# Attention values for two heads at a time, on 64 columns each, with the softmax sums added up on GpSimd

## What is computed

```python
scores = jnp.einsum('bqhd,bkhd->bhqk', q, k) * scale
attn = jax.nn.softmax(scores, axis=-1)
out = jnp.einsum('bhqk,bkhd->bqhd', attn, v)
out = out.reshape(b, t, N_HEADS * HEAD_DIM)
return out @ Wo.T
```

## Time and profile before

| | |
|---|---|
| median of three runs | 1585.21 us (1584.91 to 1586.8) |
| the profiled execution | 1585.56 us, of which the span is 1583.7 us |
| TensorE products busy | 1303.0 us, 82% of the span |
| VectorE busy | 1131.1 us, 71% |
| ScalarE busy | 755.4 us, 48% |
| GpSimd busy | 551.9 us, 35% |

### The profile page before, as it was taken

One profiled execution on the slowest core, in us unless ns is written; L12 is line 12 of the kernel. 1 busy time (PEld: TensorE's weight loads), 2 busy tenths in 40 slices (PEclk: granted clock), 3 DMA queues, 4 the chain that ended last, 5 costly groups with the idle time before them and its releaser, 6 DMA issues. The chain is left out here.

```text
span 1583.7 us, 23730 instructions
## 1 busy us (share of the span) xinstructions
PE 1303.0 (82%) x5791; PEld 914.4 (58%) x5792; DVE 1131.1 (71%) x2460; ACT 755.4 (48%) x1490; POOL 551.9 (35%) x952
## 2 busy tenths in 40 slices
PE   6499999999999999999999999999941254969600
PEld 3266666666666666666666666666631154869500
DVE  2368777788787777877788787777627784556487
ACT  1366556565565655656565565654410023333135
POOL 1101314133242323414233241322340055766548
PEclk8699999999999999999999999999955555989855
DMA  4000010110101101010110101101012012223275
GB/s 111 14 14 28 2 54 11 43 53 0 54 0 53 54 0 53 0 54 25 29 54 0 53 0 41 42 2 41 33 61 60 1 53 70 38 50 71 27 251 173
DMA packets 68357, 70.26 MB, mean 44 GB/s; under 512 B 13568, under 2 KB 64176, under 8 KB 68160
## 3 DMA queue, kind: packets, MB, share of 16 engines
q1 hardware_dynamic: 46336, 46.92, 9.9%
q10 hardware_dynamic: 16896, 16.78, 3.2%
q0 software_dynamic: 5056, 5.85, 2.4%
HBM read 40.35 MB, written 28.92 MB: 44 GB/s over the span
## 5 line engine op out<-in xcount | busy, mean ns | idle before, releaser
L824 PE MATMUL PS<-PF,V 128*128 128x512 f32 x1024 | 523.9, 593 | 0.0
L555 ACT ACTIVATE PF<-PS 128x512 f32<-128x512 f32 x512 | 303.3, 596 | 344.5 <-PE PS L750 342.9
L727 DVE TENSOR_REDUCE NMAX<-PS 128x1 f32<-128x512 f32 x512 | 346.6, 687 | 161.9 <-PE PS L759 151.8
L749 PE MATMUL PS<-Q,K 128*128 128x512 f32 x512 | 405.7, 792 | 0.9 <-ACT PF L555 0.9
L525 POOL TENSOR_TENSOR XL<-XF,XH 128x512 fp32r<-128x512 f32 x64 | 84.4, 1318 | 446.7 <-ACT XH L630 446.7
L759 PE MATMUL PS<-K,Q 128*128 128x512 f32 x512 | 203.3, 398 | 6.5 <-DVE NMAX L727 6.0
L750 PE MATMUL PS<-Q,K 128*128 128x512 f32 x512 | 202.7, 396 | 0.0
L824 PEld LDWEIGHTS PS<-PF,V 128*128 128x128 f32 x1024 | 174.4, 189 | 36.2 <-issue 7.8
L573 ACT ACTIVATE Q<-PS 64x512 fp32r<-64x512 f32 x256 | 151.6, 592 | 66.6 <-PE PS L92 61.9
L749 PEld LDWEIGHTS PS<-Q,K 128*128 128x128 f32 x512 | 97.1, 190 | 123.5 <-issue 105.4
L750 PEld LDWEIGHTS PS<-Q,K 128*128 128x128 f32 x512 | 97.3, 190 | 121.8 <-issue 121.6
(11 more groups left out here) (294 smaller groups left out, 2450.2 us busy)
## 6 DMA issues: line engine op xcount, KB each, us to landing
X<-in_L_attn_x SPq DMA_DIRECT2D x16, 512.0 KB, 5.1
MODB<-mod_rows SPq DMA_DIRECT2D x16, 512.0 KB, 4.5
h_rows<-H ACTq DMA_DIRECT2D x16, 512.0 KB, 3.1
acc_rows<-H ACTq DMA_DIRECT2D x16, 512.0 KB, 4.1
A<-acc_rows SPq DMA_DIRECT2D x16, 512.0 KB, 8.9
out_x<-X SPq DMA_DIRECT2D x16, 512.0 KB, 2.9
W1F<-in_L_ffn_W SPq DMA_DIRECT2D x3, 1024.0 KB, 4.9
W2F<-in_L_ffn_W SPq DMA_DIRECT2D x3, 1024.0 KB, 5.7
```

The source lines that it names most:

```text
L555: s_exp.done(act.activation(PF[:, u % 4, :], st_bank(u), ACT.Exp))
L727: s_mred.done(dve.tensor_reduce(NMAX[:, h % 2, c:c + 1], mx_bank(u), AX.X, ALU.max, negate=True))
L749: pe.matmul(st_bank(u), K1[:, kp, keys], Q1[:, h, :], start=True, stop=False)
L824: s_pv.done(pe.matmul(pv_bank(h), V1[:, vp, c, :], PF[:, u % 4, :], start=(c == 0), stop=(c == TC - 1)))
```

## The change

The value products are no longer issued one per slot. Every eighth slot (n = 0, 8, 16, 24), after that slot's other work, TensorE does the eight value products of a finished pair of heads: `V1` now has 64 columns only, the even head writes to rows 0 to 63 of `num_bank` and the odd head to rows 64 to 127, in turn. Two more products, with the 64 columns of `ONE` and the summed tiles `SF`, write the softmax sums of both heads to `den_bank`. GpSimd makes `SF` with three additions of 128x512 per head (`add_up`, in every slot with n % 4 not 0); the first addition of a head waits until the ones products of the pair before are done. There are eight `PF` tiles instead of four, and the exponential that follows on a pair is put behind its slot's jobs. `normalise` runs once per pair on 128 partitions instead of once per head on 64. Buffers are shared otherwise: one `XF` and one `MROW` instead of two, `YT` lies in `LTF`, and `LOWER` is made in the routing stage.

```diff
@@ PSUM banks, and the wait before a PF tile is written again
-    def pv_bank(h):
-        return PS[:, 4 + h % 2, :]
+    def values_read(eng, b, u):
+        s_pv.wait(eng, b, (TC + 1) * (u // (2 * TC)) + u % TC)
+        s_sum.wait(eng, b, (TC - 1) * (u // TC) + max(u % TC - 1, 0))
+
+    num_bank, den_bank = PS[:, 4, :], PS[:, 5, :]
@@ GpSimd
+            def add_up(b, u):
+                h, c = u // TC, u % TC
+                s_exp.wait(pool, b, u)
+                if c == 1:
+                    s_pv.wait(pool, b, (TC + 1) * (h // 2 - 1) + TC)
+                    s_sum.done(pool.tensor_tensor(SF[:, h % 2, :], PF[:, (u - 1) % (2 * TC), :], PF[:, u % (2 * TC), :], ALU.add))
+                else:
+                    s_sum.wait(pool, b, (TC - 1) * h + c - 2)
+                    s_sum.done(pool.tensor_tensor(SF[:, h % 2, :], SF[:, h % 2, :], PF[:, u % (2 * TC), :], ALU.add))
...
                 for n in range(UNITS):
+                    if n % TC and exists(b):
+                        add_up(b, n)
@@ VectorE, normalise: the four steps, now at n % 8 = 1, 2, 2, 3
-                    s_x.done(dve.transpose(RECT[:, :], bank[R:P, :]))
+                    s_x.done(dve.transpose(XF[:, :], den_bank))
...
-                    s_x.done(dve.tensor_tensor(XF[odd * R:(odd + 1) * R, p % 2, :], bank[0:R, :], RECT[:, :], ALU.mult))
+                    s_x.done(dve.tensor_tensor(XF[:, :], num_bank, XF[:, :], ALU.mult))
@@ TensorE
-                        s_exp.wait(pe, tb, u)
-                        s_pv.done(pe.matmul(pv_bank(h), V1[:, vp, c, :], PF[:, u % 4, :], start=(c == 0), stop=(c == TC - 1)))
+                    if n % 8 == 0 and exists(xb):
...
+                        for c in range(TC):
+                            for odd in range(2):
+                                rows = slice(odd * R, (odd + 1) * R)
+                                s_exp.wait(pe, xb, 2 * TC * p + TC * odd + c)
+                                last = pe.matmul(num_bank[rows, :], V1[:, vp, c, :], PF[:, TC * odd + c, :], start=(c == 0), stop=(c == TC - 1))
+                            s_pv.done(last)
+                        for odd in range(2):
+                            rows = slice(odd * R, (odd + 1) * R)
+                            s_sum.wait(pe, xb, (TC - 1) * (2 * p + odd + 1) - 1)
+                            last = pe.matmul(den_bank[rows, :], ONE[:, :], SF[:, odd, :], start=True, stop=True)
+                        s_pv.done(last)
```

More of the change, by code:

```diff
@@ L464, in body @@
                             s_mrow.wait(sp, tb, h)
-                            s_mdma.done(sp.dma_start(Q2[R:R + 1, h, :].bitcast(F32), MROW[:, h % 2, :].bitcast(F32)))
+                            s_mdma.done(sp.dma_start(Q2[R:R + 1, h, :].bitcast(F32), MROW[:, :].bitcast(F32)))
                     if n == 31 and exists(b):
@@ L547, in _, with exponent @@
         def _(act):
+            def exponent(b, u):
+                s_st.wait(act, b, u)
+                values_read(act, b, u - 2 * TC)
+                s_exp.done(act.activation(PF[:, u % (2 * TC), :], st_bank(u), ACT.Exp))
             def body(b, par):
@@ L551, in body @@
                     if exists(tb):
-                        s_st.wait(act, tb, u)
-                        s_pv.wait(act, tb, u - 4)
-                        s_exp.done(act.activation(PF[:, u % 4, :], st_bank(u), ACT.Exp))
+                        if n % 8 != 7:
+                            exponent(tb, u)
                     for job in JOBS.get(n, []):
@@ L564, in body @@
                             s_mt.wait(act, jb, idx)
-                            s_mdma.wait(act, jb, idx - 2)
-                            s_mrow.done(act.activation(MROW[:, idx % 2, :], bank[0:TC, 0:P], ACT.Copy))
+                            s_mdma.wait(act, jb, idx - 1)
+                            s_mrow.done(act.activation(MROW[:, :], bank[0:TC, 0:P], ACT.Copy))
                         elif kind == "q":
@@ L579, in body @@
                             s_vt.wait(act, jb - 1, 0)
+                            s_x1.wait(act, jb - 2, TC - 1)
                             s_latc.done(act.activation(LTF[:, :], bank, ACT.Copy))
@@ L601, in body @@
                                                       ACT.Copy))
+                    if exists(tb) and n % 8 == 7:
+                        exponent(tb, u)
                     if n == 30 and exists(b - 1):
@@ L627, in body @@
                         if exists(xb):
-                            s_x.wait(act, xb, 4 * (2 * p + 1) + 3)
+                            s_x.wait(act, xb, 4 * p + 3)
                             s_proj.wait(act, xb - 1, TC - 1)
-                            s_xhi.done(act.activation(XH[:, p, :], XF[:, p % 2, :], ACT.Copy))
+                            s_xhi.done(act.activation(XH[:, p, :], XF[:, :], ACT.Copy))
             batches(act, body)
@@ L701, in body @@
                             s_x1.wait(dve, jb, idx - 1)
+                            if idx == 0 and exists(jb + 1):
+                                s_vt.wait(dve, jb + 1, 0)
                             s_y.done(dve.tensor_tensor(YT[:, idx % 2, :], bank[:, 0:D], MODB[:, 0, :], ALU.mult))
@@ L1034, in _ @@
             dve.tensor_copy(CAND[:, 0, :].bitcast(F32), DIGU[:, 0, :].bitcast(F32)).then_inc(s_db, 1)
+            link(dve.scalar_tensor_tensor(out=LOWER[:, :], in0=DIFF[:, :], scalar=float(P), in1=SAME[:, :],
+                                          op0=ALU.is_gt, op1=ALU.mult))
             dve.wait_ge(s_exp, 2)
```

84 lines of the change are left out of this document (40 added, 44 removed).

## The result

The changed kernel takes 1672.11 us in the median of its runs (1667.11 to 1679.01); the kernel before took 1585.06 us beside it. The ratio is 1.0551, with a 95% interval from 1.0512 to 1.0590. The forecast was 1620 us: the sign was right, but the loss of 87 us is two and a half times the 35 that I expected.

What follows compares the result with a forecast made beforehand. Attention was taken as bound by TensorE. Blocks save its work, but waits make batches 69.8 us against 67.67: +2.1 us, 16 batches +34 us on 1585.56, giving 1620 us. Range 1570 to 1885 us; own case 1585 to 1680.

Steps and rivals of the forecast that it cites:

- the sign: Whole kernel: the change makes it slower, by over 0.2%, chance 0.81; faster 0.15, same 0.04.
- The block: TensorE, ten products every eight slots: two heads' products overlap, 4.7 us; rival without overlap 8.5 us, chance 0.15.
- The 0.43 us that I added: TensorE, in each block: half a product, as the odd head's first starts only behind the even head's second record.
- The load rule that I weighed: TensorE: twenty weight loads per block not hidden behind products, 3.8 us a block, 243 us in all, 1863 us; chance 0.04.
- The quarters: Four groups of eight slots per batch: 16.2, 17.9, 18.0 and 17.7 us, sum 69.8 against 67.67 before.
- The first reduction after a block: VectorE: idle until 0.90 us after each block's end, with everything behind it in its queue held.
- the reduction of slot 22: Slots 17 to 24: TensorE's L787 of slot 24 waits for it until 11.6 us; the quarter takes 18.0 us.
- `XL` behind the additions: Slots 1 to 8: `proj` of slot 6 waits behind four GpSimd additions, starts at 7.2 us; quarter 16.2 us.
- The waits: TensorE, per batch: 10.5 us of waits, 69.8 us against its own work of 59.3 us.
- GpSimd: 24 additions of 1.38 us, 33 us more per batch, 55 of 69.8 us busy; not the bound overall.
- The clock: Attention, TensorE busy 85%: a tenth less clock costs 5.9 us per batch, +95 us, 1715 us; a rival, chance 0.04.

Runs made afterwards that it cites:

- the control: VectorE's row-maximum reduction reads 64 of 512 columns, edited into the kernel before the change: 1576.63 us, ratio 0.9938.

## Why the sign was right and the size wrong

**The block.** Forecast 4.7 us, measured 4.44. That two heads overlap was right, and the run with the heads apart shows it. The 0.43 us that I added for a second head that starts half a product late does not exist: at the start of the block both heads' first products are there at once.

```profile
616.31 0.65 PE L856 MATMUL PS<-PF,V 128*64 128x512 f32 x2
```

The load rule that I weighed (the Trainium skill, TensorE: Matmul & The Clock Gate, Part 3, What overlaps and what doesn't) would have made a block 8.5 us; this trace contradicts it, the twenty loads cost nothing that shows in 4.44.

**The quarters: mis-sized.** Forecast 16.2, 17.9, 18.0 and 17.7; measured at full clock 16.2, 18.4, 19.1 and 17.4 (before: the earlier trace rows). The sum was to be 69.8 and is 71.1; the two quarters in the middle are 1.6 us short, the last is 0.3 long. The first reduction after a block is as late as I had it: VectorE stands idle until it gets the first tile, here 1.0 us after the block's end at 620.75:

```profile
621.76 0.69 DVE L755 TENSOR_REDUCE NMAX<-PS 128x1 f32<-128x512 f32 x1 [5.79 <-PE PS L787]
```

But in slots 17 to 24 I had TensorE wait for the reduction of slot 22, and it doesn't. It waits for `q` in the transpose of the maxima (1.24 us), for the exponential behind ScalarE's four `q` copies (1.38), and last for `H`, which GpSimd makes behind an addition and `XL`: that wait sets the quarter, whatever the clock or the dummies do ahead of it. I had given GpSimd no part in these slots; with small additions the quarter is 0.7 us shorter. In slots 1 to 8 I had TensorE wait for `XL` behind the additions; that wait is 0.32 us, and small additions bought 0.4. And the short reduction, which by my account should have taken the waits out of three quarters, took out 1.4 us, and 0.5 in the kernel before, which has no such waits.

**The waits.** Forecast 10.5 us a batch, 7.9 by the rows of waits, though TensorE's own work (58.3 us with a block of 4.44) leaves 12.8 of the 71.1. The difference I take to be hidden in how the rows are made: a product's modelled end reaches past the next one's start, so that gaps of 0.1 to 0.3 us are in no row of waits (L777 at 620.75 and L778 at 621.09 are 0.34 apart, not 0.23).

**GpSimd.** An addition costs 1.31 us, as L525's row gave it, and GpSimd is busy 51.9 us a batch against 55. But from a load below the batch's I took it to bind in slots 1 to 8 alone, and the additions cost 1.4 us a batch in three quarters.

**The clock: the step that failed, with the quarters.** "A tenth less clock on 59.3 us is 5.9 us per batch, +95 us: 1715 us. Against: the single waits are 1 to 3 us and dense work surrounds them. Chance 0.04." No term in the sum, and the reason against it was wrong: with waits of 0.45 to 1.4 us, and TensorE busy 63 of the 71.7 us of a batch, 82 us passed at half clock. Over the 14 batches that is about 21 us of the 70.8. My sum gave these batches 30; the 41 that it lacks are this term and the quarters above, about 20 us each. The run with the filled waits shows that the clock costs its part by itself. I had two stretches to go by the earlier trace rows, one dense and one at two thirds, took the clock to lie on a line between them, and then gave that line no weight. It should have been a term with a size, a fall or two per batch at 0.6 to 1.6 us each, not all or nothing. The Trainium skill names it (TensorE: Matmul & The Clock Gate, Part 1, A second HAM failure mode: psum-queue depth-cycling): short idle times between groups of products, over banks used in turn, can make the clock switch back and forth. This trace agrees, with its 82 us; I had weighed the other half of that page, on loads, and not this one.

**What stays open.** Which of the waits brings the clock down in a batch is not settled: filling slots 22 and 23 ended the fall there in all ten steady batches, and in six of them another came in slots 25 to 32. The split of the 70.8 us rests on profiled executions, and the one of the changed kernel is its fastest; the slower ones had a lower clock. Some 10 us in the ramps at both ends of the attention, what the short reduction gains there, and the 0.5 us a batch in the control have no cause shown.

## What to carry to other kernels

When a change turns an engine that was busy without a gap into one that waits, price the clock as well as the waits: here it was 21 us, against 50 for the waits. Price it by place: 3.4 us at half clock cost 1.6 where TensorE was the last, and 0.6 where it would have waited for GpSimd anyway. Compare variants by quarters at full clock, because a gain in one (1.4 us a batch from the small additions) can vanish in the total when the clock falls more often. Work saved on the bound engine by bunching it is worth only what the others can follow; with two banks between the engines, look for the second and third chain before the first is called the cause, and shorten two at once to see whether their gains add up. Where two half-wide products are to share the array, put them in turn, in one dense run.

## What the runs showed of the hardware

- Two products of 64 columns each, on the two halves of the columns and in turn, start together and cost 0.87 us a pair in a dense run, the price of one product of 128 columns (0.85); alone between other products a pair costs 1.01.
- Products on the two halves do not wait for one another in the order of the queue: in the block with the heads apart a product of one half started before three records of the other half that were issued ahead of it.
- The same 3.4 us at the lower clock level cost 1.6 us in slots 25-32 (18.96 against 17.38) and 0.6 in slots 17-24 (19.70 against 19.11), ahead of a wait for GpSimd.
- Dead work in the waits made the kernel 16 us faster, 1655.81 against 1672.11.
